# A post-norm attention and ternary FFN layer: keep-warm products only up to slot 9, later weight pieces, and the first keys' loads on ScalarE's queue

## The chip, the cores and the metric

The kernel runs on one core of one Trainium2 chip. The metric is the device time of one execution in microseconds (us). Engines are called PE (TensorE), DVE (VectorE), ACT (ScalarE), POOL (GpSimd) and SP (SyncE); each works through its own queue of instructions in order and waits on semaphores.

## What is computed

Sixteen sequences of 256 tokens with 256 features go through attention and a gated FFN, each followed by a residual sum and a layer norm without weights.

```python
def attn(x, Wqkv, bqkv, Wout, bout):            # 16 heads of 16, 4 groups of keys and values
    qkv = x @ Wqkv + bqkv
    q, k, v = jnp.split(qkv, [D, D + KV], axis=-1)
    k, v = tiled over the groups to 16 heads
    prob = softmax(q @ k.T / HD)
    return (prob @ v) @ Wout + bout

def ternary_quant(w, g=64):                     # both FFN weights, in groups of 64 along a row
    w = w.astype(bfloat16); w_g = w.reshape(-1, g)
    scale = clip(mean(abs(w_g)), 1e-8)
    return w + (clip(round(w_g / scale), -1, 1) * scale - w)

def ffn(x, w_gate_up, w_proj):                  # 256 -> 2 * 1024 -> 256
    gate, up = split(x @ ternary_quant(w_gate_up).T, 2)
    return rms_norm(silu(gate) * up) @ ternary_quant(w_proj).T

x = layernorm(x + attn(x)); x = layernorm(x + ffn(x))
```

## The kernel before

The kernel is one software pipeline over slots. Each sequence b takes eight slots, and every step of a sequence has an offset in slots: `Slot.once(offset)` gives the sequence whose step falls into this slot, `Slot.chunk(offset)` does so for steps that are repeated eight times (s = 0 to 7, one per slot). Sequence 0 has its x transposed in slot 1 (`X_T`), its queries projected in slot 2, its row maxima (`MAX0`) in slots 9 to 16, its exponentials (`EXP0`) in slots 15 to 22, the products with the values (`PV0`) in every other slot from 17 on, the output projection in slot 26 and the FFN from slot 31 (`FFN0`) on. Sequence 1 follows eight slots later, and so on. The first 64 slots are written out, the middle is a loop of 16 slots, and the tail is written out again; from slot 31 to the end of the loop the work of a slot repeats with a period of eight slots. Within a slot each engine runs its steps in the order of its own `slot(n)` function. For PE this is: FFN gate and up, first pair of max scores (L523), exp scores (L532), query projection (L477), second pair of max scores, products with the values (L579), key projection, the turned maxima (L592), and so on, to the turned x.

A score matmul on PE needs one of three PSUM banks `short_ps`, which DVE frees with the maximum over the row (L800, `take_maximum`). So PE's next slot begins only when DVE has taken the maxima of this one, and DVE's maxima begin only when PE has made the scores.

**The FFN weights are quantized on the chip, beside the first slots.** They come in twelve pieces. Eight hold two blocks of 128 rows of `w_gate_up` each, four hold two blocks of 128 columns of `w_proj`. A piece c goes through five steps in fixed slots:

- ACT reads it in slot `W_READ[c]` (`read_weights`: cast, abs and sign, L692 to L695); it first waits until POOL has finished piece c - 2
- DVE works on it in the slot after (`tern_weights`: the sum L821, two small ones L823 and L825, the comparison L833, and for c < `W_POOL_FROM` two multiplications L836 and L838)
- POOL finishes it in the same slot (L993 and L995; for c >= `W_POOL_FROM` the two multiplications too, L989 and L991)
- PE turns it in slot `W_TURN[c]` (L489)
- ACT copies it out of PSUM in the slot after that (`wguT` or `wpT`)

The first nine pieces (`W_LATER`) are loaded by SP ahead of everything but x, the other three in slot 4.

**Keep-warm products.** `keep_clock` puts four products of the identity with itself (L603) into each of PE's slots from `CLOCK_FROM` to `CLOCK_TO` - 1, two ahead of the turned values and two behind. Their results are never read. They go to the bank that the next piece is turned into, so they first wait for the copy of an earlier piece (`w_ev`).

**The first keys.** In slot 3 SP waits for the saved queries of sequence 0 (`q_saved`), loads its keys from DRAM into `k_st` in four DMAs (`stack_keys`, L407), and then its queries into `q_st` in eight (L399), four for each half of the heads. The first max scores, in slot 9, need the keys and the first half of the queries. The values of sequence 0 are copied by DVE in slot 7 (`v_ones`, L919), and they free the bank that the first max scores take.

## Time and profile before

| | us |
|---|---|
| median of 3 runs | 574.95 |
| lowest and highest run | 574.88 and 575.57 |
| the profiled execution | 574.5 |
| its span, first to last instruction | 571.8 |
| PE busy in the span | 528.4 (92%) |
| DVE busy | 455.4 (80%) |
| ACT busy | 374.2 (65%) |
| POOL busy | 319.5 (56%) |
| mean granted TensorE clock | 0.99 of full speed |

The time of an execution is the span and 2.7 us around it. The page divides the span into 40 slices; each digit is the busy share of a slice in tenths, and PEclk is the granted TensorE clock in tenths of full speed. In the rows further down, "[idle before <-releaser]" is how long the engine had been idle before an instruction, and what ended that idle time. "PE" rows are matmuls, "PEld" rows are weight loads that overlap them. An fp32 matmul stands as two records, so four products of the identity are "x8".

### The profile page before, as it was taken

How to read it: one execution, taken by the hardware profiler on the slowest of the kernel's cores; microseconds unless marked ns; L12 is line 12 of the kernel's file. 1: busy time of each engine (PE TensorE's matmuls, PEld its weight loads, DVE VectorE, ACT ScalarE, POOL GpSimd, SP SyncE). 2: the span in 40 equal slices, each digit the busy share in tenths (PEclk: the TensorE clock that was granted, in tenths of full speed). 3: DMA queues.
4: the chain of work that ended last, by engine and by line, in shares of the span. 5: the costliest groups of instructions: out<-in, count | busy, mean ns of one | idle time of the engine just before them, and what ended most of it. 6: DMA issues, size and time to landing. Idle time of an engine off the chain costs nothing.

```text
span 571.8 us, 13792 instructions
## 1 busy us (share of the span) xinstructions
PE 528.4 (92%) x4176; PEld 444.7 (78%) x4176; DVE 455.4 (80%) x1025; ACT 374.2 (65%) x754; POOL 319.5 (56%) x478
## 2 busy tenths in 40 slices
PE   6497999999999999999999999999999999999883
PEld 5386778778888787878888888878887877787772
DVE  6878877788888888888888887888898888885764
ACT  5456755666767767676776776776767676667663
POOL 5577671255645555555646564556555565466764
PEclk9899999999999999999999999999999999999998
DMA  7865444343333426062534444261606253010001
GB/s 229 144 142 95 86 95 104 74 91 88 84 95 93 105 68 128 19 160 26 128 69 102 93 94 100 79 116 56 134 6 166 29 125 71 12 44 6 19 20 37
DMA packets 53931, 49.05 MB, mean 86 GB/s; under 512 B 6144, under 2 KB 53888, under 8 KB 53888
## 3 DMA queue, kind: packets, MB, share of 16 engines
q1 hardware_dynamic: 53200, 48.13, 38.2%
q8 instruction: 22, 0.36, 0.3%
q10 hardware_dynamic: 688, 0.39, 0.2%
q14 instruction: 21, 0.17, 0.1%
HBM read 33.29 MB, written 14.68 MB: 84 GB/s over the span
## 4 chain that ended last, share of the span: by engine, by line
PE 63%; DVE 20%; issue 7%; POOL 4%; ACT 2%; DMA 2%; SPq 0%; DVEq 0%; ACTq 0%; POOLq 0%
PE ffn_ps L551 19%; PE short_ps L477 10%; PE pv_ps L579 8%; PE short_ps L523 8%; PE down_ps L564 7%; PE exp_ps L532 6%; DVE row_max L800 5%; DVE gated L863 3%; DVE h_f L870 3%; PE short_ps L587 2%; DVE attB L902 2%; DVE pvT L896 1%; DVE w_hat L833 1%; POOL sq_sum L966 1%; DVE w_sum L821 1%
## 5 line engine op out<-in xcount | busy, mean ns | idle before, releaser
L800 DVE TENSOR_REDUCE row_max<-short_ps 128x2 f32<-128x512 f32 x256 | 173.4, 681 | 67.2 <-PE short_ps L523 66.8
L961 POOL TENSOR_TENSOR h_lo<-h_f,h_hi 128x256 fp32r<-128x256 f32 x128 | 94.8, 740 | 206.9 <-ACT h_hi L698 206.8
L722 ACT ACTIVATE probs<-exp_ps 128x1024 f32<-128x1024 f32 x128 | 130.7, 1021 | 34.1 <-PE exp_ps L532 33.2
L523 PE MATMUL short_ps<-k_st,q_st 65*128 65x256 f32 x512 | 108.2, 294 | 9.3 <-DVE v_ones L919 6.2
L523 PEld LDWEIGHTS short_ps<-k_st,q_st 65*128 65x128 f32 x512 | 87.9, 192 | 20.7 <-issue 7.8
L707 ACT ACTIVATE tanh<-ffn_ps 128x256 f32<-128x256 f32 x120 | 45.5, 380 | 85.2 <-PE ffn_ps L551 85.2
L551 PE MATMUL ffn_ps<-x1T_hi,wguT 128*128 128x256 f32 x480 | 82.0, 293 | 10.3 <-DVE h_f L870 8.9
L564 PE MATMUL down_ps<-wpT,h_hi 128*128 128x256 f32 x256 | 78.7, 330 | 3.8 <-POOL h_lo L961 3.8
L532 PE MATMUL exp_ps<-q_st,k_st 67*128 67x512 f32 x256 | 80.7, 397 | 0.8 <-DMA q_st<-shift_lo 0.6
L551 PEld LDWEIGHTS ffn_ps<-x1T_hi,wguT 128*128 128x128 f32 x480 | 64.8, 189 | 19.3 <-issue 9.7
L966 POOL TENSOR_TENSOR sq_sum<-sq_sum,h_sq 128x256 f32<-128x256 f32 x105 | 79.5, 758 | 0.0
L551 PE MATMUL ffn_ps<-x1T_lo,wguT 128*128 128x256 f32 x480 | 78.0, 285 | 0.2 <-DVE x1T_lo L789 0.2
L579 PE MATMUL pv_ps<-probs,v_ones 128*32 128x256 f32 x1024 | 68.5, 385 | 0.3 <-DVE pvT L896 0.3
L551 PEld LDWEIGHTS ffn_ps<-x1T_lo,wguT 128*128 128x128 f32 x480 | 65.6, 190 | 1.0 <-DVE x1T_lo L789 0.4
L564 PE MATMUL down_ps<-wpT,h_lo 128*128 128x256 f32 x256 | 66.3, 281 | 0.0
L564 PEld LDWEIGHTS down_ps<-wpT,h_hi 128*128 128x128 f32 x256 | 48.5, 189 | 13.8 <-issue 7.0
L863 DVE SCALAR_TENSOR_TENSOR gated<-tanh,ffn_ps 128x256 f32<-128x256 f32 x120 | 48.8, 407 | 10.0 <-ACT tanh L707 10.0
L870 DVE TENSOR_TENSOR h_f<-gated,ffn_ps 128x256 f32<-128x256 f32 x120 | 50.5, 420 | 5.4 <-DVE gated L863 1.6
L698 ACT ACTIVATE h_hi<-h_f 128x256 fp32r<-128x256 f32 x128 | 52.3, 409 | 1.3 <-DVE h_f L870 1.3
L477 PE MATMUL short_ps<-xT,wqkv 128*128 128x256 f32 x192 | 49.1, 395 | 1.9 <-DVE shift_lo L811 1.1
L564 PEld LDWEIGHTS down_ps<-wpT,h_lo 128*128 128x128 f32 x256 | 48.6, 190 | 0.8
L762 ACT ACTIVATE h_sq<-h_f 128x256 f32<-128x256 f32 x112 | 45.7, 408 | 0.0
(102 smaller groups left out, 830.7 us busy)
## 6 DMA issues: line engine op xcount, KB each, us to landing
q_st<-q_dram SPq DMA_DIRECT2D x128, 128.0 KB, 4.1
q_dram<-q_p SPq DMA_DIRECT2D x16, 512.0 KB, 3.0
xn<-in_L_attn_x_dram SPq DMA_DIRECT2D x16, 256.0 KB, 3.4
k_st<-k_dram SPq DMA_DIRECT2D x64, 64.0 KB, 2.8
res<-in_L_attn_x_dram SPq DMA_DIRECT2D x16, 256.0 KB, 2.9
out_dram<-y_out SPq DMA_DIRECT2D x16, 256.0 KB, 2.9
wgu_raw<-in_L_ffn_w_gate_up_dram SPq DMA_DIRECT2D x8, 256.0 KB, 6.6
k_dram<-k_p SPq DMA_DIRECT2D x16, 128.0 KB, 2.4
```

What stands on the lines that cost most here:

```text
L477: last = pe.matmul(dst, a, b, start=start and i == 0, stop=stop and i == len(pairs) - 1)
L523: last = pe.matmul(bank[:, t * S:(t + 1) * S], q_st[0:PAD, st.par, head, t * P:(t + 1) * P], k_st[0:PAD, st.par, st.s % 4, :], start=True, ...
L532: last = pe.matmul(exp_ps[:, t, :], k_st[:, st.par, st.s % 4, t * P:(t + 1) * P], q_st[:, st.par, first_head(st.s):first_head(st.s) + 5:4, ...
L551: last = pe.matmul(gate_up_bank(n, st, half), wguT[:, k, c:c + P], x1T[a][:, st.par, k, :], start=first and k == 0, stop=a == 1 and k == D ...
L564: last = pe.matmul(down_ps[:, t, :], h_p[a][:, st.s % 4, t * P:(t + 1) * P], wpT[:, st.s, :], start=(st.s == 0 and t == 0 and a == 0), sto ...
L579: last = pe.matmul(pv_ps[r:r + 32, s % 4 // 2, :], v_ones[:, st.par, t, s % 4, :], probs[:, s % 4, t, i, :], start=(t == 0), stop=(t == TT ...
L722: act.activation(probs[:, st.s % 4], exp_ps[:], ACT.Exp).then_inc(exp_done, 1)
L800: dve.tensor_reduce(row_max[:, st.par, head * TT:(head + 1) * TT], short(n, f"max{i}")[:].rearrange("p (t k) -> p t k", t=TT), AX.X, ALU.m ...
L863: dve.scalar_tensor_tensor(gated[:, st.s % 2, :], tanh[:, st.s % 2, :], 1.0, gate_up_bank(n, st, 1), ALU.add, ALU.mult).then_inc(gated_don ...
L870: dve.tensor_tensor(h_f[:, st.s % 2, :], gated[:, st.s % 2, :], gate_up_bank(n, st, 0), ALU.mult).then_inc(h_done, 1)
L961: pool.tensor_tensor(h_p[1][:, st.s % 4, :], h_f[:, st.s % 2, :], h_p[0][:, st.s % 4, :].bitcast(F32), ALU.subtract).then_inc(h_lo, 1)
L966: pool.tensor_tensor(sq_sum[:, st.par, :], sq_sum[:, st.par, :], h_sq[:, st.s % 2, :], ALU.add).then_inc(h_summed, 1)
```

## The change

- The slots of the pieces: pieces 0 to 2 are read in slots 1 to 3 as before, piece 3 in slot 9 (before 5), and then one in every second slot up to 25 (before 22). The last piece is turned in slot 29 (before 26).
- The order of the pieces: they are taken as 0, 4, 1, 5, 8, 2, 6, 9, 3, 7, 10, 11 of the old list, so that the first gate and up products find their weights made first. PE no longer waits for all twelve copies ahead of the first FFN product, but for 2, 4, 7 and 10 of them at s = 0, 2, 4 and 6, and `down` waits for 5, 8, 11 and 12.
- `W_POOL_FROM` is 3 (before 4), so piece 3 has its two multiplications on POOL.
- `CLOCK_TO` is 9 (before 30): no identity products in slots 9 to 29. Five of them stand ahead of the first turned x (`CLOCK_AHEAD`).
- The four DMAs that load the keys of sequence 0 are issued by ACT, at the end of its slot 3, and no longer by SP ahead of the queries.

```diff
-W_READ = (1, 2, 3, 5, 8, 10, 12, 14, 16, 18, 20, 22)
+W_READ = (1, 2, 3, 9, 11, 13, 15, 17, 19, 21, 23, 25)
 W_MAKE = 1
-W_TURN = (5, 8, 9, 10, 12, 14, 16, 18, 20, 22, 24, 26)
+W_TURN = (5, 7, 8, 13, 15, 17, 19, 21, 23, 25, 27, 29)
 W_LATER = 9
-CLOCK_FROM, CLOCK_TO = 2, 30
-W_POOL_FROM = 4
+CLOCK_FROM, CLOCK_TO = 2, 9
+CLOCK_AHEAD = 5
+W_POOL_FROM = 3
+
+
+W_ORDER = (0, 4, 1, 5, 8, 2, 6, 9, 3, 7, 10, 11)
+GATE_UP_PIECES = (2, 4, 7, 10)
+DOWN_PIECES = (5, 8, 11, 12)
...
+        pieces = [pieces[i] for i in W_ORDER]
...
                     sp_wait(q_saved[st.par], st.count2(16, 16))
                     sp_wait(exp_scored, st.count(8, -12))
-                    if st.it is None and st.b == 0:
-                        stack_keys(st)
                     stack_queries(st, 0)
...
-                if st.it is None and st.b == 0 and st.s == 0:
-                    pe.wait_ge(w_ev, len(pieces))
+                if st.it is None and st.b == 0:
+                    pe.wait_ge(w_ev, GATE_UP_PIECES[st.s // 2])
...
                 wait(pe, h_hi, st.count(8, st.s + 1))
+                if st.it is None and st.b == 0:
+                    pe.wait_ge(w_ev, DOWN_PIECES[st.s // 2])
...
+            for _ in range(CLOCK_AHEAD):
+                pe.matmul(turn_banks[0][:, 0, 0:P], ident[:], ident[:], start=True, stop=True)
...
                 if (c := piece(n, 0)) is not None:
                     read_weights(c)
+                if n.it is None and n.t == STACK_QK:
+                    act.wait_ge(k_saved[0], 16)
+                    for c in range(4):
+                        act.dma_start(k_st[c * HD:(c + 1) * HD, 0].bitcast(F32),
+                                      k_dram[0, c % 2].rearrange("(g d) t -> d g t", d=HD)).then_inc(k_stacked[0], 16)
```

On PE the slots from the last early turned pieces to the turned maxima of slot 13 read as follows. First before, from the piece turned in slot 8 (`down_ps<-ident_bf,w_hat`) on; L523 are max scores, L587 and L477 the turned x and the projections of sequence 1, L603 the identity products, L489 a turned piece:

```order
L489 MATMUL down_ps<-ident_bf,w_hat 128x128 x4
L523 MATMUL short_ps<-k_st,q_st 128x256 x4
L603 MATMUL ffn_ps<-ident 128x128 x4
L587 MATMUL short_ps<-ident,xn 128x128 x4
L489 MATMUL ffn_ps<-ident_bf,w_hat 128x128 x4
L523 MATMUL short_ps<-k_st,q_st 128x256 x2
L477 MATMUL short_ps<-xT,wqkv 128x256 x4
L523 MATMUL short_ps<-k_st,q_st 128x256 x2
L603 MATMUL down_ps<-ident 128x128 x4
L489 MATMUL down_ps<-ident_bf,w_hat 128x128 x4
L523 MATMUL short_ps<-k_st,q_st 128x256 x4
L603 MATMUL ffn_ps<-ident 128x128 x4
```

And after (the line numbers are a few higher: L528 max scores, L594 and L482 turned x and projections, L610 identity products, L494 a turned piece):

```order
L494 MATMUL down_ps<-ident_bf,w_hat 128x128 x4
L610 MATMUL ffn_ps<-ident 128x128 x4
L494 MATMUL ffn_ps<-ident_bf,w_hat 128x128 x4
L528 MATMUL short_ps<-k_st,q_st 128x256 x4
L594 MATMUL short_ps<-ident,xn 128x128 x4
L528 MATMUL short_ps<-k_st,q_st 128x256 x2
L482 MATMUL short_ps<-xT,wqkv 128x256 x4
L528 MATMUL short_ps<-k_st,q_st 128x256 x10
L482 MATMUL short_ps<-xT,wqkv 128x256 x2
```

The third piece has moved ahead of the first max scores, the fourth and the identity products are gone from between the scores, and the scores of slots 10 to 12 stand ten in a row.

On DVE the same slots, before, from the comparison of piece 3 on; L821 to L838 are the work on a piece, L919 the copied values, L800 the row maxima:

```order
L833 TENSOR_TENSOR w_hat<-w_abs,w_half 128x512
L836 TENSOR_TENSOR w_hat<-w_hat,w_scale 128x512
L838 TENSOR_TENSOR w_hat<-w_hat,w_sign 128x512
L919 COPY v_ones<-short_ps 128x4x16 x2
L800 TENSOR_REDUCE row_max<-short_ps 128x2 x2
L821 TENSOR_REDUCE w_sum<-w_abs 128x8
L823 TENSOR_SCALAR w_scale<-w_sum 128x8
L825 TENSOR_SCALAR w_half<-w_scale 128x8
L833 TENSOR_TENSOR w_hat<-w_abs,w_half 128x512
L800 TENSOR_REDUCE row_max<-short_ps 128x2 x4
```

And after, from the comparison of piece 2 on (L836 to L853 are the work on a piece, L934 the copied values, L815 the maxima):

```order
L848 TENSOR_TENSOR w_hat<-w_abs,w_half 128x512
L851 TENSOR_TENSOR w_hat<-w_hat,w_scale 128x512
L853 TENSOR_TENSOR w_hat<-w_hat,w_sign 128x512
L934 COPY v_ones<-short_ps 128x4x16 x2
L815 TENSOR_REDUCE row_max<-short_ps 128x2 x4
L836 TENSOR_REDUCE w_sum<-w_abs 128x8
L838 TENSOR_SCALAR w_scale<-w_sum 128x8
L840 TENSOR_SCALAR w_half<-w_scale 128x8
L848 TENSOR_TENSOR w_hat<-w_abs,w_half 128x512
L815 TENSOR_REDUCE row_max<-short_ps 128x2 x4
```

The work on piece 3 stood ahead of the values and the first maxima, and stands now behind the maxima of slot 10, with four instructions where it had six. Behind the first maxima there were eight pieces, and there are nine now.

On ACT, from the second piece's sign on, before:

```order
L695 ACTIVATE w_sign<-w_bf 128x512
L692 ACTIVATE w_bf<-wgu_raw 128x512
L694 ACTIVATE w_abs<-w_bf 128x512
L695 ACTIVATE w_sign<-w_bf 128x512
L692 ACTIVATE w_bf<-wgu_raw 128x512
L694 ACTIVATE w_abs<-w_bf 128x512
L695 ACTIVATE w_sign<-w_bf 128x512
L698 ACTIVATE wguT<-ffn_ps 128x2x256
```

And after:

```order
L705 ACTIVATE w_sign<-w_bf 128x512
L702 ACTIVATE w_bf<-wgu_raw 128x512
L704 ACTIVATE w_abs<-w_bf 128x512
L705 ACTIVATE w_sign<-w_bf 128x512
L778 DMA k_st<-k_dram 16x4x256 x4
L708 ACTIVATE wguT<-ffn_ps 128x2x256
L708 ACTIVATE wguT<-down_ps 128x2x256
```

The four loads of the keys stand behind the third piece's sign, in the place where the fourth piece was read.

## Rows read from the trace of the kernel before

**Rows 1.** The page's first line.

```profile
span 571.8 us, 13792 instructions
```

**Rows 2.** Busy time by stage: span, PE, PEld, DVE, ACT, POOL, clock, DMA share, GB/s.

```profile
31.30:56.12 24.82, 20.28 (x158) 17.30 (x157) 20.49 (x40) 15.94 (x27) 19.32 (x18) 1.00 0.54 114
56.12:82.23 26.11, 24.97 (x212) 20.16 (x213) 22.06 (x44) 16.93 (x27) 19.80 (x18) 1.00 0.46 98
82.23:110.24 28.01, 26.87 (x217) 22.17 (x218) 19.95 (x44) 15.76 (x26) 6.37 (x11) 1.00 0.45 92
```

**Rows 3.** The chain that ended last, 25.9 to 27.6 us: start, length, what.

```profile
25.93 0.42 DVE w_hat L838
...
26.36 0.28 DVE v_ones L919 x2
...
26.77 0.78 PE short_ps L523 x2
```

**Rows 4.** Timeline, all engines: start, length, engine, operation, count, idle before.

```profile
6.27 5.10 PE L477 MATMUL short_ps<-xT,wqkv 128*128 128x256 f32 x12 [0.69 <-ACT xT L698]
...
9.36 0.19 ACT L730 ACTIVATE bq_s<-bq 128x2 f32<-128x2 f32 x1
...
10.15 0.84 ACT L735 ACTIVATE q_f<-short_ps,bq_s 128x256 f32<-128x256 f32 x2 [0.60 <-PE short_ps L477]
...
20.48 0.40 PE L489 MATMUL down_ps<-ident_bf,w_hat 128*128 128x128 bf16 x4 [1.06 <-POOL w_hat L995]
...
31.30 1.97 PE L477 MATMUL short_ps<-xT,wqkv 128*128 128x256 f32 x8
```

**Rows 5.** One-microsecond windows around the fall and the rise of the clock, columns as in 2.

```profile
22.00:23.00 1.00, 0.00 (x0) 0.00 (x0) 0.80 (x2) 0.81 (x2) 0.76 (x1) 1.00 1.16 132
24.00:25.00 1.00, 0.00 (x0) 0.00 (x0) 1.00 (x1) 0.28 (x1) 0.62 (x1) 0.75 1.15 131
31.00:32.00 1.00, 1.00 (x5) 0.86 (x5) 0.50 (x1) 0.65 (x2) 0.92 (x2) 0.84 1.09 301
```

**Rows 6.** Timeline of SP, the loads of the first keys and queries.

```profile
17.84 1.75 SPq L407 DMA_DIRECT2D k_st<-k_dram  x4
19.63 3.74 SPq L399 DMA_DIRECT2D q_st<-q_dram  x8
```

**Rows 7.** Landing times of the third and fourth query load, issued at 20.6 and 21.0 us.

```profile
L399 SPq DMA_DIRECT2D q_st<-q_dram x2: 430/430/431, 20.6 to 21.0; - x2
...
DMA to landing us min/median/max: 4.1/4.4/4.7
```

**Rows 8.** Timeline of POOL: the last operation on piece 2.

```profile
23.46 1.16 POOL L995 TENSOR_TENSOR w_hat<-w_hat,w_bf 128x512 bf16<-128x512 bf16 x1
```

**Rows 9.** Groups of DVE by shape, 26.8 to 98.2 us: busy, mean ns, idle before.

```profile
L800 DVE TENSOR_REDUCE row_max<-short_ps 128x2 f32<-128x512 f32 x44 | 29.1, 682 | 12.0 <-PE short_ps L523 11.8
L833 DVE TENSOR_TENSOR w_hat<-w_abs,w_half 128x512 bf16<-128x512 bf16 x8 | 6.4, 798 | 0.3
L821 DVE TENSOR_REDUCE w_sum<-w_abs 128x8 f32<-128x512 bf16 x8 | 5.4, 675 | 0.6 <-ACT w_sign L695 0.6
L823 DVE TENSOR_SCALAR w_scale<-w_sum 128x8 bf16<-128x8 f32 x8 | 2.7, 338 | 0.3
L825 DVE TENSOR_SCALAR w_half<-w_scale 128x8 bf16<-128x8 bf16 x8 | 2.3, 289 | 0.3
```

**Rows 10.** The chain again: scores, and the first and last of six identity bursts.

```profile
64.76 0.89 PE ffn_ps L603 x8
...
65.87 0.29 PE short_ps L523 x2
...
95.23 0.89 PE ffn_ps L603 x8
```

**Rows 11.** Timeline: maxima behind sequence 3's query projection; the first FFN product on x1T_lo.

```profile
84.47 0.69 DVE L800 TENSOR_REDUCE row_max<-short_ps 128x2 f32<-128x512 f32 x1 [2.05 <-PE short_ps L523]
...
98.18 0.75 PE L551 MATMUL ffn_ps<-x1T_lo,wguT 128*128 128x256 f32 x4 [0.20 <-DVE x1T_lo L789]
```

## The prediction

> **What bounds the kernel now.** The edits touch only the first 31 slots, so the first thing to read is where these end and what follows. The first FFN product on the low half of x1 runs at 98.2 us [rows 11]; from there the program is the same word for word, and every slot repeats with a period of eight. So the change is worth what it moves this point, and nothing else. The second view is the busy time by stage [rows 2]. From 56.1 to 82.2 us (slots 18 to 25) PE is busy for 25.0 of 26.1 us, and DVE for 22.1. It looks like a bound by PE. But PE's busy time holds the identity products: one burst of four takes 0.89 us [rows 10], and there is one per slot, so 7.1 of the 25.0 us are filling. The real work of PE is 17.9 us in eight slots, and DVE, with 22.1, is the engine behind it. The third view is the chain of waits. Up to 26.8 us it runs through the quantized weights on ACT, DVE and POOL, and its last links there are DVE's sixth operation on piece 3, the copied values and then the first max scores [rows 3]. Behind it, to 98 us, the chain changes between PE's scores and DVE's maxima, and six bursts of identity products lie on it, from 64.8 to 95.2 us, 0.89 to 1.09 us each [rows 10], about 5.5 us in all. The fourth view is DVE's groups between the first maxima and slot 31: its 44 row maxima waited 12.0 us in sum, 11.8 of it for PE [rows 9]. That idle time is what can be won behind the first scores.
>
> **Up to the first max scores.** They start at 26.77 us, right behind the values, which stood behind piece 3 on DVE [rows 3]. With piece 3 gone to slot 10, DVE comes to the values sooner by the six operations of that piece. What is late next? Two things. First, PE now turns piece 2 in slot 8, ahead of the scores, and waits for POOL's last operation on it, which ends at 23.46 + 1.16 = 24.6 us [rows 8]; a turned piece takes 0.40 us [rows 4], so 25.0 us. Queued behind this wait on PE are the first scores, and behind them DVE's first maxima. Second, the fourth query load, issued at 21.0 us, landed 4.7 us later, at 25.7 us [rows 7]. SP spent 17.84 to 19.63 us on the keys' loads first [rows 6], so without them each query load is issued 1.8 us earlier, and the fourth would land at 23.9 us. That is the lower bound, since the keys' loads now run beside them. The upper bound comes from the bytes: in this stretch the DMA engines are full (share 1.16) at 132 GB/s [rows 5], and the keys are 4 x 64 KB, which is 2.0 us at that rate, so 25.9 us. The Trainium skill speaks here, on its page "DMA: Bandwidth & Descriptors", section "Issuing engines are not separate DMA queues": transfers started by different engines run on the same 16 DMA engines and interleave. The full share agrees; by that rule alone a second issuer saves only the time to issue, and the sum would stay at the 25.9 us end. I take 25.0 us, where the middle of the two bounds, 24.9 us, and POOL's piece 2 meet. On ACT the four issues take about what they took on SP, 1.75 us [rows 6], and they lie in the time in which ACT would wait for the next piece. So the first scores gain **1.8 us**, with bounds of 0.9 (25.9 us) and 2.4 (24.4 us, if the whole weight chain also starts 0.6 us earlier).
>
> That start is the matter of the five products ahead of the first x. PE's first projections took 5.10 us for 12 records, and the same form later 1.97 us for 8 [rows 4]: 425 against 246 ns each, so the first ones ran near half speed, although the granted clock is given as full there. If the array is at full speed sooner, they end about 1 us sooner. But ACT is busy with piece 0 until 9.36 + 0.19 = 9.55 us, and it began on the queries at 10.15 us [rows 4], so at most 0.6 us of this passes on. In the other direction five products at the low level take some 2.2 us behind the identity (twice 0.89 / 4 each) and could hold x back by 0.1 to 0.2 us. I take 0.2 us of gain, inside the 1.8.
>
> **From the first scores to slot 31.** The change takes out 21 bursts of identity products (slots 9 to 29), 21 x 0.89 = 18.7 us of PE's time. Only what lies on the chain can come back: 5.5 us, the six bursts. Against it, DVE has one more piece behind the first maxima, nine where eight stood. A piece costs it 798 + 675 + 338 + 289 ns = **2.1 us** [rows 9], now without its two multiplications, which are POOL's. DVE is the engine that is late next, so I put these 2.1 us fully on the path. And where a burst goes, the next thing is not at hand at once: in a slot with a piece DVE comes to the maxima later than PE to the scores. Walking through slots 26 to 30 with the durations of the rows, DVE is late in nearly every slot behind the output projection, since pieces 10 and 11 are now made in slots 24 and 26. The waits for the query projections stay as well: the maxima of slot 26 waited 2.05 us for it [rows 11], and there is one such in slots 10, 18 and 26. I take 1.8 us of the 5.5 as lost so. This stretch then gains 5.5 - 2.1 - 1.8 = **1.6 us**, with bounds of -0.5 (DVE takes all but the piece) and 3.4 (all six bursts come back).
>
> **The other edits** I cost at nothing. The new order of the pieces and the split waits of gate, up and down: the last piece is copied in slot 30, and the earliest product that needs any is in slot 31, so no wait is ever open; the cover is gone only if PE comes to slot 31 before ACT has passed slot 30. SP's later queue moves with the rest. POOL has the two multiplications of piece 3 more (2.3 us by the one in [rows 8]), in slot 10, where it would wait. One wait is new at the end: the four operations on piece 11 (4 x 1.16 = 4.6 us) stand in slot 26 ahead of the first layer norm's statistics in slot 27; ACT's x1, PE's turned x1 in slot 29 and all of PE's slot 30 are queued behind these. My walk has PE there about 0.5 us early, and that is inside the 1.8 us.
>
> **The sum.** 1.8 + 1.6 = 3.4 us. The span goes from 571.8 [rows 1] to 568.4 us, and the profiled execution, 2.7 us more, from 574.5 to 571.1. It lies 0.45 us under the median of the runs, so for the median I forecast 574.95 - 3.4, **571.5 us**.
>
> **The clock, which the products were there for.** PE had turned a piece at 20.48 us and then did nothing [rows 4, 5]; the granted clock fell from 2.4 to 1.2 GHz at about 24.5 us, and came back at about 31.3 us, after PE had worked without a gap from 26.8 [rows 5]. With the change PE is idle from about 21.4 to 24.6, so I expect the same fall and the same first query projection at the low level. Once back, the level is at risk again in slots 11 to 14: two pairs of scores of 0.29 us [rows 10] in a slot of some 2.7 us leave PE busy for a fifth. No stretch of this trace is that thin without being idle, so it can't be read off. The Trainium skill, page "TensorE: Matmul & The Clock Gate", section "Part 1: The HAM clock gate", states that the throttled state is the default and activity releases it. This is a rule against the change.
>
> **Rivals.** (A) As summed: 570.6 to 572.6 us, chance 0.38. (B) The clock falls in slots 11 to 14 and returns by slot 17, as it did after some 4.5 us of dense work. DVE is late there anyway, but the exp scores of slot 15 and the scores of slots 16 and 17 stand at the low level in front of the maxima. That costs about 2 us (four pairs of scores and two exp scores, at 0.29 and about 0.5 us more each): 573.5 us, 572.6 to 574.2, chance 0.24. (C) The clock doesn't fall in front of slot 9, or returns before slot 10's query projection, which takes 1.97 us at the high level [rows 4] and about 3.5 at the low one; DVE's maxima behind it move by 1.3 us more, and the bursts come back nearly whole: 568.5 to 570.4 us, 0.15. (D) The identity products only filled idle time of PE, so taking them out does nothing, and DVE's extra piece eats the gain at the start: 1.8 - 2.1 + 0.5, 574 to 575.6 us, 0.13. For it: DVE is busy for 22.1 of 26.1 us [rows 2]. Against it: six bursts stand on the chain. (E) Slower: the clock stays at the low level in slots 16 to 29, since PE, with the products gone, has only 17.9 us of work in 26.1. At the low level this work is 35.8 us in eight slots against 26.1 now, 1.2 us a slot more than before. From the third such slot on the gain of 3.4 us is gone; six give 574.95 - 3.4 + 6 x 1.2 = 578.8 us, all fourteen 588.4. Against it: at the low level PE would be packed, as from 26.8 to 31.3 us, and there the clock rose. Chance 0.10, 576 to 589 us.
>
> **The numbers.** (A) is likeliest: 571.5 us. About 0.2% (1.15 us) is what a measurement of this kernel can tell from no change. Faster by more than that holds (A), (C) and most of (B): 0.73. Within: the rest of (B) and most of (D), 0.16. Slower: (E) and a little of (D), 0.11. The range from 568.8 to 575.0 us leaves out (E) and the outer ends of (C) and (D).
>
> **What would show it.** The first max scores at about 25.0 us (26.77 before), ended by POOL's piece 2 or a landing, not by the values. The first FFN product on x1T_lo at about 94.8 us (98.18 before), and nothing gained or lost after it. DVE's sum in front of its maxima up by one piece and their idle time down from 12.0 to about 8 to 9 us. The granted clock in windows from 32 to 50 us: full for (A), half for (B), half beyond 60 us for (E). Wrong would be the whole forecast if PE were the slower one of the pair even without the bursts.

## The result and the profile after

The changed kernel takes 580.9 us (median of four runs, 579.2 to 584.5) against 574.9 us before. The ratio is 1.0105, with a 95% interval of 1.0075 to 1.0135: it is about 6 us slower, where 3.4 us of gain were forecast. The profiled execution took 584.5 us, the longest of the four, so what is read from its trace overstates the median by some 3.6 us. Its page:

```profile
span 582.7 us, 13474 instructions
...
PEclk9765857799999999999999999999999999999997
```

The same row of the kernel before:

```profile
PEclk9899999999999999999999999999999999999998
```

The span is 10.9 us longer than in [rows 1]. The time grew by 10.0 us only, since 1.8 us lie around the span here and 2.7 us did before. The first FFN product on x1T_lo starts at 109.05 us, 10.9 us later than in [rows 11], so all of the difference lies in front of slot 31, and nothing changes behind it. The row of the granted clock has changed: from the second to the eighth of the 40 slices it stands at 5 to 8 tenths, where the kernel before is below 9 tenths in the second and the last slice only.

The start went much as forecast. Timeline of the changed kernel, all engines (start, length, engine, operation, idle before and what ended it):

```profile
6.33 2.86 PE L482 MATMUL short_ps<-xT,wqkv 128*128 128x256 f32 x12 [0.69 <-ACT xT L708]
...
9.46 0.84 ACT L745 ACTIVATE q_f<-short_ps,bq_s 128x256 f32<-128x256 f32 x2
...
23.23 1.15 POOL L1010 TENSOR_TENSOR w_hat<-w_hat,w_bf 128x512 bf16<-128x512 bf16 x1
...
24.43 0.40 PE L494 MATMUL ffn_ps<-ident_bf,w_hat 128*128 128x128 bf16 x4 [2.85 <-POOL w_hat L1010]
...
25.35 0.71 PE L528 MATMUL short_ps<-k_st,q_st 65*128 65x256 f32 x4 [0.52 <-DMA q_st<-q_dram]
...
28.50 3.75 PE L482 MATMUL short_ps<-xT,wqkv 128*128 128x256 f32 x8 [0.35 <-ACT xT L708]
```

With the five products ahead of the first x, the first projections took 2.86 us for 12 records instead of 5.10, and ACT began on the queries at 9.46 instead of 10.15 us [rows 4]. POOL ends piece 2 at 24.4 us, PE turns it, and the first max scores start at 25.35 us, ended by the landing of a query load. Before it was 26.77 us [rows 3]: 1.4 us gained, 1.8 forecast. The first query projection then runs at the low level, 3.75 us for 8 records.

Behind it everything is later. The stages between the query projections of slots 10, 18, 26 and 34, columns as in [rows 2] (the first begins at the max scores behind slot 10's projection):

```profile
31.69:57.58 25.89, 19.76 (x83) 14.50 (x81) 20.62 (x39) 12.56 (x21) 18.70 (x17) 0.58 0.44 94
57.58:88.17 30.59, 26.57 (x150) 17.83 (x149) 23.59 (x48) 19.87 (x31) 21.54 (x19) 0.67 0.42 84
88.17:120.71 32.54, 29.16 (x188) 22.00 (x188) 22.50 (x48) 17.26 (x30) 10.57 (x15) 0.79 0.36 78
```

Slots 18 to 25 take 30.6 us where they took 26.1, and slots 26 to 33 take 32.5 where they took 28.0. In these two stages PE's busy time has grown in spite of the products that are gone; the granted clock is 0.67 and 0.79 on average. In this trace PE waits for DVE at three places, each behind a piece in an even slot, and near each of them the clock falls. First the three waits, and the first FFN product behind them:

```profile
36.81 0.80 PE L528 MATMUL short_ps<-k_st,q_st 65*128 65x256 f32 x2 [2.84 <-DVE row_max L815]
...
68.10 1.94 PE L586 MATMUL pv_ps<-probs,v_ones 128*32 128x256 f32 x16 [1.24 <-DVE pvT L911]
...
94.30 0.57 PE L528 MATMUL short_ps<-k_st,q_st 65*128 65x256 f32 x2 [2.43 <-DVE r L940]
...
109.05 0.74 PE L556 MATMUL ffn_ps<-x1T_lo,wguT 128*128 128x256 f32 x4
```

Then the windows of one microsecond in which the clock falls, and one inside each of the low stretches, columns as in [rows 2]:

```profile
36.00:37.00 1.00, 0.19 (x1) 0.19 (x2) 1.00 (x3) 0.00 (x0) 0.77 (x1) 0.78 0.87 295
67.00:68.00 1.00, 0.00 (x0) 0.00 (x0) 0.97 (x3) 0.50 (x1) 1.00 (x1) 0.64 0.48 128
94.00:95.00 1.00, 0.70 (x3) 0.70 (x4) 0.96 (x3) 0.00 (x0) 0.92 (x2) 0.80 0.95 327
37.00:57.00 20.00, 16.79 (x70) 12.19 (x71) 16.19 (x32) 8.86 (x15) 16.17 (x15) 0.50 0.50 98
68.00:87.00 19.00, 17.10 (x93) 11.23 (x94) 14.55 (x32) 9.12 (x13) 13.61 (x13) 0.50 0.57 98
95.00:108.00 13.00, 13.00 (x69) 8.76 (x68) 7.14 (x17) 6.08 (x10) 4.54 (x7) 0.50 0.37 66
```

At 36.8 us PE had waited 2.84 us for a row maximum that stood behind piece 3 (slot 10). At 68.1 us it had waited 1.24 us for the transposed values, which stood behind the piece of slot 20. At 94.3 us it had waited 2.43 us for the sum behind the output projection, which stood behind piece 11 in slot 26. The clock fell at 36.6, 67.3 and 94.6 us, and came back at 57.0, 87.8 and 108.2 us. In the low stretches PE is busy for 84, 90 and 100% of the time, and still they last 20.4, 20.5 and 13.6 us.

Neither the falls nor the lengths are fixed. In a second execution of the same kernel (e13 below) the clock is low from 23.8 to 58.0 and from 71.6 to 88.7 us, and full behind that. There the last two of the three waits are these:

```profile
69.82 1.07 PE L586 MATMUL pv_ps<-probs,v_ones 128*32 128x256 f32 x16 [2.34 <-DVE pvT L911]
...
94.68 0.51 PE L528 MATMUL short_ps<-k_st,q_st 65*128 65x256 f32 x2 [1.38 <-DVE r L940]
```

And this is the window of the second one, columns as in [rows 2]:

```profile
94.00:95.00 1.00, 0.32 (x2) 0.32 (x3) 0.96 (x3) 0.00 (x0) 1.00 (x1) 1.00 0.00 0
```

So the waits for the values and for the sum are there with the clock full too, and no fall follows the second of them.

The maxima of DVE, by contrast, now wait for PE:

```profile
L815 DVE TENSOR_REDUCE row_max<-short_ps 128x2 f32<-128x512 f32 x44 | 29.1, 683 | 21.6 <-PE short_ps L528 21.6
```

21.6 us of waiting in 44 maxima, where it was 12.0 [rows 9].

### The profile page after: what moved, and what is told of

Read it like the earlier page. It is cut to its first block, busy times and chain, and to the rows that moved or that the text cites. A ratio compares the mean times of both kernels' runs of the same rounds, so it can differ in the third digit from the quotient of the medians.

```text
span 582.7 us, 13474 instructions
## 1 busy us (share of the span) xinstructions
PE 535.0 (92%) x4018; PEld 442.3 (76%) x4018; DVE 455.0 (78%) x1023; ACT 374.0 (64%) x754; POOL 321.9 (55%) x480
## 3 DMA queue, kind: packets, MB, share of 16 engines
q1 hardware_dynamic: 52880, 47.86, 37.7%
## 4 chain that ended last, share of the span: by engine, by line
PE 64%; DVE 21%; issue 8%; DMA 3%; POOL 2%; ACT 1%; SPq 0%; DVEq 0%; ACTq 0%; POOLq 0%
PE ffn_ps L556 19%; PE short_ps L482 9%; PE pv_ps L586 9%; PE short_ps L528 8%; PE exp_ps L537 7%; PE down_ps L571 7%; DVE row_max L815 5%; DVE gated L878 3%; DVE h_f L885 3%; PE short_ps L594 3%; DVE attB L917 2%; DVE pvT L911 2%; DMA q_st<-q_dram 1%; DVE w_hat L848 1%; POOL sq_sum L981 1%
## 5 line engine op out<-in xcount | busy, mean ns | idle before, releaser
L815 DVE TENSOR_REDUCE row_max<-short_ps 128x2 f32<-128x512 f32 x256 | 173.4, 681 | 76.8 <-PE short_ps L528 76.8
L976 POOL TENSOR_TENSOR h_lo<-h_f,h_hi 128x256 fp32r<-128x256 f32 x128 | 94.6, 739 | 207.3 <-ACT h_hi L708 207.2
L528 PE MATMUL short_ps<-k_st,q_st 65*128 65x256 f32 x512 | 115.0, 312 | 8.1 <-DVE row_max L815 3.0
L528 PEld LDWEIGHTS short_ps<-k_st,q_st 65*128 65x128 f32 x512 | 94.6, 207 | 23.3 <-DVE row_max L815 3.5
L556 PE MATMUL ffn_ps<-x1T_hi,wguT 128*128 128x256 f32 x480 | 82.1, 293 | 10.3 <-DVE h_f L885 8.9
L537 PE MATMUL exp_ps<-q_st,k_st 67*128 67x512 f32 x256 | 86.0, 419 | 2.1 <-ACT probs L732 2.0
L586 PE MATMUL pv_ps<-probs,v_ones 128*32 128x256 f32 x1024 | 73.7, 409 | 2.1 <-DVE pvT L911 2.1
L571 PEld LDWEIGHTS down_ps<-wpT,h_hi 128*128 128x128 f32 x256 | 48.6, 190 | 13.6 <-issue 7.0
L482 PE MATMUL short_ps<-xT,wqkv 128*128 128x256 f32 x192 | 50.4, 402 | 1.0 <-ACT xT L708 1.0
L586 PEld LDWEIGHTS pv_ps<-probs,v_ones 128*32 128x32 f32 x1024 | 28.0, 114 | 24.7 <-issue 4.6
```

What stands on the lines that cost most here:

```text
L482: last = pe.matmul(dst, a, b, start=start and i == 0, stop=stop and i == len(pairs) - 1)
L528: last = pe.matmul(bank[:, t * S:(t + 1) * S], q_st[0:PAD, st.par, head, t * P:(t + 1) * P], k_st[0:PAD, st.par, st.s % 4, :], start=True, ...
L537: last = pe.matmul(exp_ps[:, t, :], k_st[:, st.par, st.s % 4, t * P:(t + 1) * P], q_st[:, st.par, first_head(st.s):first_head(st.s) + 5:4, ...
L556: last = pe.matmul(gate_up_bank(n, st, half), wguT[:, k, c:c + P], x1T[a][:, st.par, k, :], start=first and k == 0, stop=a == 1 and k == D ...
L571: last = pe.matmul(down_ps[:, t, :], h_p[a][:, st.s % 4, t * P:(t + 1) * P], wpT[:, st.s, :], start=(st.s == 0 and t == 0 and a == 0), sto ...
L586: last = pe.matmul(pv_ps[r:r + 32, s % 4 // 2, :], v_ones[:, st.par, t, s % 4, :], probs[:, s % 4, t, i, :], start=(t == 0), stop=(t == TT ...
```

## The experiments

Times are medians. The runs before were 575.3 us beside the first four kernels, 575.5 beside the next four, 575.6 beside the third four and 576.6 beside the last four. The ratio is not in every row the quotient of the two medians (e5: 1.0002, with 576.7 against 575.5 us). "Low" is the time at the 1.2 GHz level up to the end of slot 31, read from windows of one microsecond; "slot 31" is the start of the first FFN product on x1T_lo. These two are from the one profiled execution, and executions of one kernel differ: the changed kernel has 109.1 and 105.0 (e13), the old slots 96.2 (e7) and 97.8 (e14).

| run | time | ratio to before (95%) | slot 31 | low |
|---|---|---|---|---|
| before | 574.9 | | 98.2 | 6.8 |
| the changed kernel | 580.9 | 1.0105 (1.0075 to 1.0135) | 109.1 | 64.7 |
| e1 changed, products to slot 29 | 579.4 | 1.0073 (1.0049 to 1.0097) | 101.1 | 13.7 |
| e2 before, products to slot 8 | 573.3 | 0.9963 (0.9947 to 0.9980) | 97.6 | 34.2 |
| e3 changed, half the products | 580.8 | 1.0083 (1.0058 to 1.0108) | 105.5 | 40.8 |
| e4 before, keys on ACT | 575.4 | 0.9992 (0.9975 to 1.0010) | 100.0 | 17.0 |
| e5 changed, pieces one slot earlier | 576.7 | 1.0002 (0.9974 to 1.0031) | 102.2 | 47.8 |
| e6 before, pieces 4 to 11 in even slots | 581.3 | 1.0115 (1.0073 to 1.0158) | 103.0 | 17.1 |
| e7 changed, old slots | 573.0 | 0.9955 (0.9929 to 0.9981) | 96.2 | 27.2 |
| e8 as e5, products to slot 29 | 577.2 | 1.0036 (1.0020 to 1.0053) | 102.4 | 20.5 |
| e9 as e6, piece behind the norm | 576.6 | 1.0025 (1.0011 to 1.0040) | 105.3 | 23.8 |
| e10 changed, piece behind the norm | 580.4 | 1.0092 (1.0068 to 1.0116) | 103.8 | 47.9 |
| e11 as e7, products to slot 15 | 574.8 | 0.9984 (0.9962 to 1.0007) | 98.7 | 23.8 |
| e12 as e7, last piece two slots later | 575.7 | 1.0001 (0.9984 to 1.0018) | 100.9 | 37.7 |
| e13 changed, again | 580.7 | one run | 105.0 | 51.3 |
| e14 as e7, again | 573.4 | 0.9948 (0.9920 to 0.9977) | 97.8 | 37.6 |
| e15 before, again | 576.0 | one run | 99.0 | 10.2 |
| e16 changed, light pieces | 573.9 | 0.9954 (0.9933 to 0.9974) | 97.6 | 41.1 |

**The first theory was the clock alone:** without products it falls, and everything else is forecast right. The rival was the order of the work.

e1:

```diff
-CLOCK_FROM, CLOCK_TO = 2, 9
+CLOCK_FROM, CLOCK_TO = 2, 30
```

> The changed kernel with CLOCK_TO back at 30: four identity products in each of the slots 9 to 29, everything else as changed. Theory 1 (the clock): the changed kernel lost its time because the granted clock stood at the low level for some 61 us between 26 and 108 us. With the products back the clock should be full from about 33 us on, the first FFN product on x1T_lo at 96 to 98 us, and the time 572.5 to 575.5 us: the first scores keep their 1.4 us, and DVE's extra piece takes up to 2.1 of it. Theory 2 (the order): the moved pieces, DVE's ninth piece and POOL's late operations in front of the first layer norm cost the time, and the clock only follows PE's waiting. Then the time stays at 578 us or above whatever the clock does.

e2, the reverse on the kernel before:

```diff
-CLOCK_FROM, CLOCK_TO = 2, 30
+CLOCK_FROM, CLOCK_TO = 2, 9
```

> The kernel before with CLOCK_TO = 9 alone: no identity products in slots 9 to 29. Theory 1 (the clock): the same low stretches as in the changed kernel, 577 to 586 us. Theory 2 (the order): without the moved pieces nothing is lost, and the six bursts on the chain come back, 570 to 575 us.

Both went against the first theory. With all products back the changed kernel takes 579.4 us: 1.5 us less, with intervals that overlap. The kernel before without them is faster than with them, by 0.37%, though in its trace it stands at the low level five times as long. Of its 1.9 us, 1.1 lie in the span (medians of the spans 571.5 against 572.6 us); 0.8 us lie around it, where the kernel before has 2.6 us at the median and e2 1.8. No run shows what these are. Its windows, columns as in [rows 2], a wait, and its first FFN product:

```profile
40.00:41.00 1.00, 0.94 (x4) 0.94 (x5) 0.39 (x2) 0.24 (x1) 1.00 (x1) 0.54 0.42 130
57.00:58.00 1.00, 1.00 (x6) 0.90 (x6) 0.30 (x1) 0.75 (x1) 0.92 (x2) 0.92 0.03 6
```

```profile
40.06 1.17 PE L523 MATMUL short_ps<-k_st,q_st 65*128 65x256 f32 x4 [2.93 <-DVE row_max L800]
...
97.62 0.73 PE L551 MATMUL ffn_ps<-x1T_lo,wguT 128*128 128x256 f32 x4 [0.21 <-DVE x1T_lo L789]
```

Low from 40.1 to 57.2 us, and yet slot 31 comes 0.6 us sooner. The wait of 2.93 us for a row maximum, behind the piece of slot 11, is as long as the 2.84 us of the changed kernel at 36.8 us: with the pieces in the old slots and the products gone it is there as well, so the moved pieces did not bring it. The loss is tied to the moved pieces. In e1 the trace names a place for it, the products with the values in slots 21 and 25:

```profile
67.42 1.07 PE L586 MATMUL pv_ps<-probs,v_ones 128*32 128x256 f32 x16 [1.58 <-DVE pvT L911]
...
80.74 1.07 PE L586 MATMUL pv_ps<-probs,v_ones 128*32 128x256 f32 x16 [1.39 <-DVE pvT L911]
```

PE waits 1.58 and 1.39 us for the transposed values. Before, only the second such product waited, for 0.28 us. The clock does not fall at either of them in e1 (granted 1.00 from 66 to 70 and from 80 to 82 us), so such a wait costs time without a fall. The profiled execution of e1 was the shortest of six (577.1 us). DVE does a piece ahead of the normalization within a slot, and slots 20 and 24 had no piece before.

e3 halves the products (`keep_clock(n, 2 if n.t < 9 else 1)`, up to slot 29):

> The changed kernel with two identity products a slot in slots 9 to 29, where the kernel before has four. Theory 1: if two are enough to keep the clock, the time is 1 to 4 us under that of the run with four (569 to 573 us); if not, there are low stretches again and 575 to 581 us. Theory 2 has nothing change by more than 1 us against the changed kernel (580 to 582 us).

580.8 us: no better than none. Half the products don't hold the clock, which is low for 40.8 us. The number lies in what either theory allowed, so this run does not tell them apart.

e4 moves the keys' loads alone:

```diff
-                    if st.it is None and st.b == 0:
-                        stack_keys(st)
...
+                if n.it is None and n.t == STACK_QK:
+                    act.wait_ge(k_saved[0], 16)
+                    for c in range(4):
+                        act.dma_start(k_st[c * HD:(c + 1) * HD, 0].bitcast(F32), ...
```

> The kernel before with the first keys' four loads issued by ACT alone. The queries land up to 1.8 us earlier, but the first scores stood behind the copied values at 26.6 us, which stand behind piece 3 on DVE. So the first scores stay at 26.7 to 26.8 us and the time at 574.5 to 575.5 us. If instead the loads held the first scores, these come at about 25.5 us and the time is 573.5 us.

575.4 us, no change, and the first scores at 26.60 us, as expected.

**The second theory was the parity of the slots.** Its rival was the number of pieces behind the first maxima and their late end.

e5 and e8 (e8 has `CLOCK_TO = 30` too):

```diff
-W_READ = (1, 2, 3, 9, 11, 13, 15, 17, 19, 21, 23, 25)
+W_READ = (1, 2, 3, 8, 10, 12, 14, 16, 18, 20, 22, 24)
-W_TURN = (5, 7, 8, 13, 15, 17, 19, 21, 23, 25, 27, 29)
+W_TURN = (5, 7, 8, 12, 14, 16, 18, 20, 22, 24, 26, 28)
```

> The changed kernel with pieces 3 to 11 read one slot earlier (slots 8, 10, ... 24) and turned one slot earlier (12, 14, ... 28): DVE works on them in the odd slots 9 to 25, nine pieces behind the first maxima as in the changed kernel, no identity products from slot 9 on. Theory parity: in even slots a piece stands on DVE between the maxima of a slot with a long projection on PE (10, 18, 26) and, in slots 20 and 24, ahead of the values' normalization, for which PE's products of slots 21 and 25 wait. Then most of the loss goes: 572 to 576 us. Theory count: the ninth piece (2.1 us) and the late end of the pieces cost it, 579 us or more, as in the changed kernel.

> As the run with the pieces one slot earlier, and with the four identity products per slot up to slot 29. Theory parity: the first scores keep 1.4 us, the ninth piece takes up to 2.1: 573 to 576.5 us, and 1 to 3 us slower than without the products if these only lie in the way of the scores. Theory count: 578 us or more.

e6, on the kernel before:

```diff
-W_READ = (1, 2, 3, 5, 8, 10, 12, 14, 16, 18, 20, 22)
+W_READ = (1, 2, 3, 5, 9, 11, 13, 15, 17, 19, 21, 23)
-W_TURN = (5, 8, 9, 10, 12, 14, 16, 18, 20, 22, 24, 26)
+W_TURN = (5, 8, 9, 10, 13, 15, 17, 19, 21, 23, 25, 27)
```

> The kernel before, with its identity products, and only pieces 4 to 11 read and turned one slot later: DVE works on them in the even slots 10 to 24, still eight behind the first maxima. Theory parity: 577 to 580 us, as in the changed kernel with the products back (579.4). Theory count: 574.5 to 576 us, no change.

e7, the changed kernel with `W_READ`, `W_TURN` and `W_POOL_FROM` of the kernel before:

> The changed kernel with the slots of the pieces and W_POOL_FROM as before: it keeps the new order of the pieces, the products stopped at slot 9, five of them ahead of the first x, and the keys' loads on ACT. If the slots of the pieces are all that costs time, this is as the kernel before with the products stopped at slot 9 (573.3 us), within 1.5 us. If the products ahead of x, the order of the pieces or the keys' loads cost something, it is above 575 us.

e6 decides that the place counts: the same eight pieces, the same products, one slot later, and 5.8 us more than before (581.3 us, where 577 to 580 were expected). Its products with the values, and its first FFN product:

```profile
67.95 1.18 PE L579 MATMUL pv_ps<-probs,v_ones 128*32 128x256 f32 x16 [1.58 <-DVE pvT L896]
...
81.92 1.49 PE L579 MATMUL pv_ps<-probs,v_ones 128*32 128x256 f32 x16 [1.68 <-DVE pvT L896]
...
103.02 0.74 PE L551 MATMUL ffn_ps<-x1T_lo,wguT 128*128 128x256 f32 x4 [0.20 <-DVE x1T_lo L789]
```

The two waits are 1.58 and 1.68 us, and the clock falls at 68.8 and 82.4 us, right behind each of them; neither fall is in a trace of the kernel before. e6 is low for 10.3 us more than before, so the clock can be only a part of its 5.8 us. e5 takes back 4.2 us of the changed kernel's 6. That is not parity alone, since its last piece also leaves slot 26, where it stood ahead of the sum, and its 576.7 us (573.1 to 579.2) lies between the two ranges expected. e8, at 577.2 us, lies between its two ranges too, and 0.4 us over e5 tells nothing about the products. e7 says that the slots of the pieces are the whole of the loss: with the old ones the other edits give 573.0 us, as much as e2 within 0.4 us, so the products ahead of x, the order of the pieces, the split waits and the keys' loads are together worth nothing that can be measured. It is faster than both kernels, and so it was when run again:

> The version with the old slots of the pieces and everything else as changed, once more on another day of the chip: 572 to 574 us, faster than the kernel before by 0.3 to 0.6%, if the gain is real.

573.4 us, 0.52% under the kernel before. Of the differences of the medians, 2.5 and 3.2 us, 1.8 and 2.0 us lie in the span.

What is left, 576.7 (e5) against 573.0 us (e7), is the ninth piece and the late end.

e12, e7 with the last piece two slots later:

```diff
-W_READ = (1, 2, 3, 5, 8, 10, 12, 14, 16, 18, 20, 22)
+W_READ = (1, 2, 3, 5, 8, 10, 12, 14, 16, 18, 20, 24)
-W_TURN = (5, 8, 9, 10, 12, 14, 16, 18, 20, 22, 24, 26)
+W_TURN = (5, 8, 9, 10, 12, 14, 16, 18, 20, 22, 24, 28)
```

> The old slots of the pieces without products from slot 9 on (573.0 us), and only the last piece two slots later: read in 24, made in 25, turned in 28. Eight pieces stand behind the first maxima as before. If the late end (a piece on DVE and four operations on POOL in front of the first layer norm) is what makes nine pieces in odd slots cost 3.7 us, this gives 575 us or more. If the number of pieces does, it is as without it, 572.5 to 574 us.

575.7 us: 2.7 of the 3.7 us come with the late last piece. So, in steps of medians: 573.0 (e7), + 2.7 for the late last piece, + 1.0 to e5 with the ninth piece, + 4.2 for the step to even slots, 580.9 us. The step of 1.0 us is less than either kernel scatters (573.0 to 576.5 and 573.1 to 579.2 us), so a price of the ninth piece is not shown.

The traces of e12 and e14 show where the late piece costs. Both have some 37.6 us at the low level, and they are level at 82.2 us. Slot 26's query projection and what follows, in e12:

```profile
85.02 3.68 PE L482 MATMUL short_ps<-xT,wqkv 128*128 128x256 f32 x8 [1.25 <-DVE shift_lo L826]
...
88.12 1.15 POOL L1010 TENSOR_TENSOR w_hat<-w_hat,w_bf 128x512 bf16<-128x512 bf16 x1
...
88.79 1.89 PE L482 MATMUL short_ps<-wo,attT 128*128 128x256 f32 x8
...
92.66 0.20 POOL L985 TENSOR_TENSOR ve<-mv,ln_eps 128x2 f32<-128x2 f32 x1 [1.02 <-DVE mv L947]
```

And in e14:

```profile
83.64 1.97 PE L482 MATMUL short_ps<-xT,wqkv 128*128 128x256 f32 x8
85.68 1.89 PE L482 MATMUL short_ps<-wo,attT 128*128 128x256 f32 x8
```

In e12 the last piece stands on DVE in slot 25 ahead of the shift that PE waits for. The projection starts 1.4 us later, the clock falls at 85.1 us, and it takes 3.7 instead of 2.0 us; slot 31 is then 3.1 us later. POOL has long ended its four operations when the layer norm needs it. They are not what costs here.

**Where the even slots cost.** Two rivals: the values' normalization, or the long projections. e9 and e10 turn the order round within a DVE slot, e9 on e6 and e10 on the changed kernel:

```diff
-                if (c := piece(n, W_MAKE)) is not None:
-                    tern_weights(c)
                 if st := n.once(SHIFT_SPLIT[1]):
...
                         dve.transpose(attT[:, half, :], attB[:]).then_inc(att_turned, 1)
+                if (c := piece(n, W_MAKE)) is not None:
+                    tern_weights(c)
                 if st := n.once(O_ADD):
```

> The kernel before with pieces 4 to 11 in the even slots 10 to 24 (the run that took 581.3 us) and one thing more: within a slot DVE does the piece behind the values' normalization instead of ahead of it. Theory normalization: the even slots cost their 6 us because PE's products of slots 21 and 25 wait for the transposed values (1.6 and 1.7 us) behind the pieces of slots 20 and 24; with the order turned round the waits are gone, and the time is 575 to 578 us. Theory projections: they cost it because the pieces of slots 10, 12, 18 and 20 stand between the maxima that PE's long projections release and the next ones; then the time stays above 579.5 us.

> The changed kernel with the same one edit: the piece behind the values' normalization within a DVE slot. Theory normalization: 576 to 578.5 us instead of 580.9. Theory projections: 580 us or more.

The two disagree. With the products (e9) the turn wins 4.7 of 5.8 us, 576.6 us, as the first rival had it. Its profiled execution was the longest of ten (582.4 us), so its trace is no guide to the median. Without the products, in the changed kernel, it wins 0.5 us, which is nothing. The wait for the values is gone from e10's trace, but the piece of slot 20 now stands ahead of the next slot's shift, and PE waits for that:

```profile
70.53 0.50 PE L528 MATMUL short_ps<-k_st,q_st 65*128 65x256 f32 x2 [2.11 <-DVE shift_lo L826]
```

The waits of 2.69 us for a row maximum at 36.9 us and of 2.38 us for the sum at 92.7 us are still there. So in the changed kernel it isn't shown which of the places costs how much.

e11 asks whether products in slots 9 to 15, where PE has little to do, pay for themselves (`CLOCK_TO = 16` on e7):

> The old slots of the pieces, the other edits as changed, and the identity products up to slot 15 instead of slot 8 (the run that stopped at slot 9 took 573.0 us). In slots 9 to 15 PE has little work and waits for DVE, so products there should cost little and could keep the clock full up to the dense slots: 571 to 573 us. If they lie in the way as the later ones do, or if the clock falls later anyway, 573 to 575.5 us.

574.8 us, 571.8 to 576.7: not better than none, and the clock fell at 48.0 us all the same. The executions spread over 4.9 us.

**The clock's price.** Two kernels were run again unchanged.

> The changed kernel once more, unchanged, for a second execution with its trace. If the low clock itself is what costs time, this execution lies on one line with the first (span 582.7 us with 64.7 us at the low level between 10 and 110 us): about 0.35 us less for each us less at the low level. If the waits for DVE cost it and the clock only follows, the first FFN product on x1T_lo stays within 1.5 us of 109 us whatever the low stretches are.

> The kernel before once more, for a second trace. With the identity products PE is nearly always busy, so a longer low stretch should cost more per us than in the changed kernel: about 0.4 to 0.5 us for each us at the low level beyond the 6.8 us of the first trace.

The moments at which the clock falls differ between executions of one kernel. Pages' first lines and first FFN products of e13 and e15:

```profile
span 578.9 us, 13474 instructions
...
104.95 0.74 PE L556 MATMUL ffn_ps<-x1T_lo,wguT 128*128 128x256 f32 x4
```

```profile
span 573.1 us, 13792 instructions
...
98.98 0.74 PE L551 MATMUL ffn_ps<-x1T_lo,wguT 128*128 128x256 f32 x4 [0.20 <-DVE x1T_lo L789]
```

With the order fixed, e13 has 13.4 us less at the low level than the first trace of the changed kernel (51.3 against 64.7) and a span 3.8 us shorter: 0.28 us for each. e15 has 3.4 us more than the first trace of before and a span 1.3 us longer: 0.38. e14 has 10.4 us more than e7 and a span 1.6 us longer: 0.15. The four timed executions of the changed kernel side with the first two:

| time | span | mean granted clock |
|---|---|---|
| 584.53 | 582.7 | 0.938 |
| 580.76 | 578.9 | 0.945 |
| 581.04 | 579.2 | 0.945 |
| 579.23 | 577.4 | 0.950 |

As an estimate, a mean of 0.938 is 2 x 0.062 x 582.7 = 72 us at the low level, one of 0.950 is 58 us: 5.3 us of span for 14.5 us, 0.36 each. But among ten executions of e12 one of 573.9 us has a mean clock of 0.958 and one of 576.5 us has 0.961, and in e5 573.1 and 577.5 us stand at 0.956 and 0.958. So time at the low level goes with a longer span in most of these kernels, at 0.15 to 0.38 us per us, and it does not account for all of their scatter. That e13's first FFN product comes 4.1 us sooner than in the first trace speaks for a price of the clock. That it is still 7.2 us later than in e14, which has the old slots and 13.7 us less at the low level, is more than the 2.1 to 5.2 us that these would cost at that price, so by this estimate the order costs as well.

The last run (e16) leaves out most of DVE's part of pieces 3 to 11, that is the sum and the two operations on w_scale and w_half behind it, with their waits; these pieces are then scaled with old numbers, so the result is not the right one:

```diff
+                if c < 3:
                     dve.tensor_reduce(w_sum[:], w_abs[:, c % 2], AX.X, ALU.add).then_inc(w_red, 1)
...
```

> The changed kernel without the sum, the scale and its half on DVE for pieces 3 to 11 (the output is not the reference's, since these pieces are scaled with an earlier piece's numbers): DVE's part of a piece is one operation of 0.7 us instead of 2.1 us. If DVE's pieces open the gaps on PE in which the clock falls, the low stretches between 36 and 108 us shrink from 54 to under 30 us and the time goes to 566 to 572 us, well more than the 4 us by which it would fall if only the durations counted. If missing products alone let the clock fall, the low stretches stay and the time is 576 us or more.

573.9 us, 7.0 us less than the changed kernel, which lies between the two ranges expected. (By the ratios to the runs beside them it is 1.5%, or 8.7 us.) The clock is low for 41.1 us in front of slot 31, not for under 30 as expected, so low time stays without these waits, as it does in e2 and e7. The waits for the values and for the sum are gone or under 0.8 us, though PE waits 1.43 us for ACT's x1 at 94.8 us, and the clock falls at 72.2 and 96.1 us for 3.4 us each. The first FFN product comes at 97.6 us, 11.4 us sooner than in the first trace of the changed kernel and 7.3 us sooner than in e13. DVE has 11.3 us less work by the changed kernel's own rows (9 x (676 + 410 + 170) ns):

```profile
L836 DVE TENSOR_REDUCE w_sum<-w_abs 128x8 f32<-128x512 bf16 x9 | 6.1, 676 | 0.0
L838 DVE TENSOR_SCALAR w_scale<-w_sum 128x8 bf16<-128x8 f32 x9 | 3.7, 410 | 0.3
L840 DVE TENSOR_SCALAR w_half<-w_scale 128x8 bf16<-128x8 bf16 x9 | 1.5, 170 | 0.3
```

As an estimate at 0.15 to 0.38 us each, the 10.2 us less at the low level than in e13 are worth 1.5 to 3.9 of the 7.3 us, and the 23.6 us less than in the first trace 3.5 to 9.0 of the 11.4. The rest, between 2 and 8 us, is then DVE's time and what waits for it. This division is worked out, not shown: no run holds the clock fixed with the order changed.

## Why the prediction was wrong

**Up to the first scores: right.** 1.4 us against 1.8, held by a query landing 0.5 us behind POOL's piece 2, inside the bounds.

**From the first scores to slot 31: wrong in sign.** "I take 1.8 us of the 5.5 as lost so. This stretch then gains 5.5 - 2.1 - 1.8 = 1.6 us". Measured in the profiled executions, it lost 12.3 us (slot 31 is 10.9 us later although the scores start 1.4 us sooner), and in the second trace (e13) 8.4 us (6.8 us later, the scores 1.6 us sooner). The step that failed is the price of DVE's pieces: one more piece at 2.1 us and the others, moved, at nothing. The late last piece and the clock failed beside it.

- *DVE's extra piece at 2.1 us.* It was counted as work of one kind, wherever it stands. The step looked at how many pieces there are and not at what stands behind each of them. The moved slots put a piece in front of the transposed values (slots 20 and 24) and of the sum in slot 26, and PE waits for them: 1.24 and 2.43 us in the first trace, 2.34 and 1.38 us in e13, where the kernel before has 0.28 us at most for the values and e2 and e7 0.56 us for the sum. The wait of 2.84 us for a row maximum behind piece 3 does not belong to it, since e2 and e7 have 2.93 us with the old slots. With eight pieces, and nothing else changed, the even slots cost 5.8 us (e6), and putting the piece behind the values' normalization takes 4.7 of them back (e9). Without the products the same turn takes back 0.5 us only (e10), so for the changed kernel the division among the places stays open. The forecast named the even slots 24 and 26 and priced them at nothing more than DVE being late.
- *The late last piece at nothing.* The forecast looked at POOL's four operations on it: "My walk has PE there about 0.5 us early, and that is inside the 1.8 us." With the piece in slot 25 that holds: POOL is free in time (e12). With it in slot 26, POOL starts the layer norm's first small operation at 99.8 us in e13, some 4 us behind DVE's statistics, and PE waits 0.76 us for ACT's x1. What cost 2.7 us in e12 was DVE's part of the piece, which the forecast didn't walk through there: the shift behind it, PE's projection 1.4 us later, and that projection at the low level.
- *The clock.* It was given 2 us as a case of its own, (B), and the case that came closest, (E), a chance of 0.10. The argument against (E) was that PE would be packed at the low level and the clock would rise, as between 26.8 and 31.3 us. It was nearly packed, busy for 84, 90 and 100% of the three stretches, and the clock stayed low for 20 us at a time. The first stretch, back at 57.0 us, ends where (B) had it, at slot 17. (E)'s price, 1.2 us a slot, gives 588 us for all fourteen slots where 584.5 was profiled, but that it comes near is in part luck: e2 and e7 are low for 34 and 27 us and lose nothing, so a low clock by itself is not the loss, and (E) knew nothing of the moved pieces.

**The six bursts on the chain** were right in sign for the kernel before: taking the products out, and nothing else, wins 1.9 us (e2), 1.1 of them in the span, and not the 3.7 us that 5.5 - 1.8 give. The clock is low for 27 us longer there, which may be why. With the pieces in the new slots the same edit gains nothing that can be measured: 580.9 against 579.4 us (e1), 576.7 against 577.2 us (e5, e8). So rival (D) is wrong for the old order and not refuted for the new one. The keys' loads at nothing were right (e4), and so, as far as e7 can tell, were the split waits.

**The time around the span** was carried over at 2.7 us and is 1.8 us.

**The range** (568.8 to 575.0 us) left (E) out. What would have caught it is in the order of the two programs: which DVE instruction stands behind each moved piece, and which PE instruction waits for that.

What stays open is how the 7.9 us between e7 and the changed kernel divide between the waits themselves and the clock. The 37.5 us more at the low level between their first traces are, at 0.15 to 0.38 us each, 5.6 to 14 of the 12.9 us at slot 31. Between their second traces (e13 and e14) it is 13.7 us more, worth 2.1 to 5.2 of 7.2 us. That the waits make the clock fall isn't shown. In the first trace of the changed kernel and in e6 falls stand within 1 us of them, but e1 has two such waits and e13 one (1.38 us) without a fall, in e7 PE waits 1.95 us for ACT up to 63.5 us with the clock full and it stays full until 72.7 us, and runs without products in the old slots fall as well, at 38.6 to 40.7 us (e2, e7, e12, e14) and at 64.0 to 64.6 us (e2, e12, e14).

## What to carry over

Before moving side work on an engine to other slots, list for each new place what that engine does next and who waits for it; one slot's shift with the same amount of work cost 1% here, and turning the order round within the slot won most of it again (e9). Work that only keeps a clock up is to be tried without, in the old order, before anything else is moved: it was worth taking out there (0.4 to 0.5%), and nothing else in this change was worth anything. Two traces of one kernel can differ by 4 us here, so a place named by one trace is to be looked for in a second. A forecast with an engine that is left a third idle has to price the lower clock as likely, not as a tail.

## What was not expected of the hardware

- At the low level PE was busy for 84 to 100% of 20.4, 20.5 and 13.6 us without the clock coming back sooner (36.6 to 57.0, 67.3 to 87.8 and 94.6 to 108.2 us in the changed kernel), where in the kernel before 4.5 us of work without a gap were followed by the rise.
- A wait of PE is no sure sign of a fall. With the clock full, one of 1.24 us stood beside a fall (67.3 us, changed kernel), and in e1 one of 1.59 us (42.2 us). Waits of 1.23 and 1.16 us in the kernel before (39.8 and 45.0 us), of 1.58 and 1.39 us in e1, of 1.38 us in e13 and of 1.95 us in e7 were passed over.
- The same program falls at different moments in different executions: 24.5 and 24.2 us, and then either not at all or at 48.1 us, in the two traces of the kernel before; at 36.6, 67.3 and 94.6 us, or low already from 23.8 and again at 71.6 us, in the two of the changed kernel. The four executions of the changed kernel spread over 5.3 us.
- The low level costs less than its half speed suggests: 0.15 to 0.38 us of span for each us, by three pairs of traces.
- Small operations of DVE can stretch: w_scale on 128x8 took 1.18 us at 34.0 us in the changed kernel, where it takes 0.17 us elsewhere in the same trace (91.5 us). POOL ran an operation of 1.26 us over the same stretch (from 33.9 us). That this is the cause is argued from the overlap alone.
